# AdaLN-conditioned feed-forward layer on one core: first batch's chain in another order, first weight group halved, small vectors loaded as rows, token parameters on GpSimd

## The reference

```python
attn_in = jnp.tanh(jnp.einsum('bsd,da->bsa', hidden, W1) + b1)     # A = 128
scores = jnp.einsum('bsa,a->bs', attn_in, v)
mask = jnp.where(pt == 0, l <= j, jnp.where(pt == 1, l >= j, l != j))
p = softmax(where(mask, scores[:, None, :], -1e30))
pooled = jnp.einsum('bjl,bld->bjd', p, hidden) / mask.sum(-1)
h = (pooled - mu) * rsqrt(var + 1e-5) * ln_gamma + ln_beta
y = silu(h @ w1 + fc1_bias)          # w1 = (fc1_q - 128) * scales, 512 x 2048
z = y @ w2 + fc2_bias                # w2 = (fc2_q - 128) * scales, 2048 x 512
out = x + pooled + 0.5 * z
```

## Time and profile before

| | us |
|---|---|
| median of 3 runs | 1687.94 |
| lowest, highest | 1685.69, 1688.06 |
| profiled execution | 1684.57 |
| its span in the profile | 1682.8 |
| TensorE busy | 1644.5 (98%) |
| VectorE busy | 931.1 (55%) |
| ScalarE busy | 422.6 (25%) |
| GpSimd busy | 177.6 (11%) |

### The profile page before, as it was taken

How to read it: one execution, slowest core, us unless ns; L and a number is a source line. 1 busy time by engine, 2 the same in 40 slices (tenths; PEclk the granted TensorE clock), 3 DMA queues, 4 the chain that set the end, 5 groups by cost and what they waited for, 6 DMA issues and landing times.

```text
span 1682.8 us, 20819 instructions
## 1 busy us (share of the span) xinstructions
PE 1644.5 (98%) x7648; PEld 1310.1 (78%) x7648; DVE 931.1 (55%) x1827; ACT 422.6 (25%) x632; POOL 177.6 (11%) x140
## 2 busy tenths in 40 slices
PE   4699999999999999999999999999999999999999
PEld 2578878787887878878788787878878788787887
DVE  8887464655546565464564546555365554645612
ACT  2442232223122232222222222231221322222210
POOL 1202010020200102011020200102011020110200
PEclk7799999999999999999999999999999999999999
DMA  9500001010010100101000010100101001010000
GB/s 271 191 1 24 27 1 50 1 51 1 1 52 0 51 1 1 52 1 51 1 33 19 1 50 1 52 1 1 51 1 52 1 1 51 1 51 1 26 0 26
DMA packets 29679, 52.39 MB, mean 31 GB/s; under 512 B 5888, under 2 KB 6400, under 8 KB 29056
## 3 DMA queue, kind: packets, MB, share of 16 engines
q1 hardware_dynamic: 28608, 50.62, 9.1%
q10 hardware_dynamic: 960, 0.27, 0.1%
HBM read 34.10 MB, written 16.78 MB: 30 GB/s over the span
## 4 chain that ended last, share of the span: by engine, by line
PE 95%; DVE 3%; DMA 1%; issue 0%; ACT 0%; SPq 0%; DVEq 0%
PE z_ps L826 14%; PE z_ps L827 14%; PE z_ps L828 14%; PE y_ps L813 14%; PE y_ps L814 14%; PE y_ps L815 14%; PE a_ps L797 2%; PE a_ps L719 2%; PE a_ps L736 1%; DMA fc_scaled<-in_L_ffn_fc_scales_dram 1%; PE a_ps L789 1%; PE a_ps L738 1%; PE a_ps L786 1%; PE a_ps L737 1%; PE a_ps L788 1%; PE a_ps L787 1%
## 5 line engine op out<-in xcount | busy, mean ns | idle before, releaser
L826 PE MATMUL z_ps<-w_hi,y_hi 128*128 128x512 f32 x1024 | 418.9, 409 | 0.0
L813 PE MATMUL y_ps<-hT_hi,w_hi 128*128 128x512 f32 x1024 | 406.2, 397 | 3.0 <-DVE hT_lo L629 2.7
L827 PE MATMUL z_ps<-w_lo,y_hi 128*128 128x512 f32 x1024 | 406.9, 397 | 0.0
L828 PE MATMUL z_ps<-w_hi,y_lo 128*128 128x512 f32 x1024 | 403.6, 394 | 0.0
L814 PE MATMUL y_ps<-hT_lo,w_hi 128*128 128x512 f32 x1024 | 402.9, 394 | 0.0
L815 PE MATMUL y_ps<-hT_hi,w_lo 128*128 128x512 f32 x1024 | 401.3, 392 | 0.0
L412 ACT ACTIVATE y_f<-y_ps,b 128x512 f32<-128x512 f32 x256 | 176.0, 687 | 884.9 <-PE y_ps L815 884.9
L652 DVE CAST y_hi<-y_f 128x512 fp32r<-128x512 f32 x256 | 120.2, 469 | 269.0 <-PE z_ps L828 222.2
L826 PEld LDWEIGHTS z_ps<-w_hi,y_hi 128*128 128x128 f32 x1024 | 192.5, 188 | 61.6 <-issue 19.2
L813 PEld LDWEIGHTS y_ps<-hT_hi,w_hi 128*128 128x128 f32 x1024 | 192.7, 188 | 49.5 <-issue 3.7
L828 PEld LDWEIGHTS z_ps<-w_hi,y_lo 128*128 128x128 f32 x1024 | 192.3, 188 | 46.5
(11 more groups left out here) (142 smaller groups left out, 1146.2 us busy)
## 6 DMA issues: line engine op xcount, KB each, us to landing
x<-in_x_dram SPq DMA_DIRECT2D x64, 256.0 KB, 3.6
out_dram<-x SPq DMA_DIRECT2D x64, 256.0 KB, 2.2
fc_codes<-in_L_ffn_fc_q_dram SPq DMA_DIRECT2D x8, 1024.0 KB, 15.0
fc_scaled<-in_L_ffn_fc_scales_dram SPq DMA_DIRECT2D x8, 1024.0 KB, 16.5
scratch<-in_L_cond_W_dram ACTq DMA_DIRECT2D x1, 256.0 KB, 3.7
b2h<-in_L_ffn_fc_bias_dram SPq DMA_DIRECT2D x1, 256.0 KB, 8.1
tok_i<-in_itok_B_dram ACTq DMA_DIRECT2D x1, 8.0 KB, 5.5
v_col<-in_L_cond_v_dram ACTq DMA_DIRECT2D x1, 0.5 KB, 6.0
```

The lines of the kernel that those rows point to most:

```text
L813: mm(o, w1_hi[:, c, cols], hT_hi[:, c, :], start=(c == 0), stop=False)
L826: mm(z_ps[r][:], y_hi[k % 2][:, rows], w2_hi[:, k, :], start=(k == 0), stop=False)
L827: mm(z_ps[r][:], y_hi[k % 2][:, rows], w2_lo[:, k, :], start=False, stop=False)
L828: last = mm(z_ps[r][:], y_lo[k % 2][:, rows], w2_hi[:, k, :], start=False, stop=(k == NF - 1))
```

## The change

- First batch, x: transposed tile by tile (J) instead of by column block, so that each tile's x^T can be split as soon as it has come. The projection is made in two halves of 256 columns, in two banks, tanh and scores as well. The scans read the scores in PSUM. The scores as a column come from four small matmuls (`score_columns`) instead of a product with the identity.
- First batch, rest: ScalarE makes the high parts of x (XSH), with `xs_hi` and `y_hi` as buffers; the exponential for the sums (EXPE) starts after COLS; the other exponentials in two steps with a semaphore count each, in all batches, and PC's halves release TensorE one by one. h is transposed tile by tile into `z_ps`, and fc1's blocks 0 and 1 are made together, column block by column block (`fc1_first_pair`).
- Weights: five groups, of 2, 2, 4, 4 and 4 blocks (w1 groups 0 to 4, w2 groups 5 to 9). D and W of w1's groups 0 and 1 stand behind the pooling, L of group 0 after H, everything of w2 in the FFN.
- Small vectors: five transfers put gamma, beta, fc1's bias, v and b1 as 26 rows of 128 into `vec_rows`; one transpose and one copy give `vec_cols`.
- Queues: `wc_f` and the tokens move to SyncE, behind x.
- GpSimd makes the token parameters, and `bias` waits for the splits of h (`hT_done`) instead of h.

The diff's core:

```diff
-    NG = NF // ND
+    GROUPS = ((0, 2), (2, 4), (4, 8), (8, 12), (12, 16))
...
-        DVE_LATE = {0: [("D", 1)], 1: [("D", 5)], 2: [("L", 1)], 3: [("D", 2), ("L", 5)], 4: [("D", 6)], 5: [("L", 2)],
-                    6: [("L", 6)], 15: [("D", 3)], 16: [("D", 7)], 17: [("L", 3)], 19: [("L", 7)]}
+        DVE_LATE = {0: [("D", 2)], 1: [("D", 6)], 2: [("L", 2)], 3: [("L", 6), ("D", 7)], 4: [("D", 3)],
+                    5: [("L", 7), ("D", 8)], 6: [("L", 3)], 7: [("L", 8)], 15: [("D", 4)], 16: [("D", 9)],
+                    17: [("L", 4)], 19: [("L", 9)]}
...
             def bias(a, p, J):
                 pool.wait_ge(res_added, a * NJ + (J + 1))
                 if J == 0:
-                    pool.wait_ge(h_ready, a * NJ + NJ)
+                    pool.wait_ge(hT_done, a * ND + ND)
...
-            act.dma_start(wc_f.rearrange("p (c a) -> p c a", c=ND), cond_w.rearrange("(c p) a -> p c a", p=P)).then_inc(wc_in, 16)
-            act.dma_start(tok_i[:], itok.rearrange("(o d) -> o d", o=1).to_broadcast([P, B])).then_inc(tok_in, 16)
-            act.dma_start(v_col[:], cond_v.rearrange("(p o) -> p o", o=1)).then_inc(cond_in, 16)
-            act.dma_start(b1c[:], cond_b.rearrange("(p o) -> p o", o=1)).then_inc(cond_in, 16)
+            rows = [(gamma, 0, ND), (beta, ND, ND), (fc1_b, 2 * ND, NF), (cond_v, 2 * ND + NF, 1), (cond_b, 2 * ND + NF + 1, 1)]
+            for vector, r0, n in rows:
+                act.dma_start(vec_rows[r0:r0 + n, :], vector.rearrange("(c p) -> c p", p=P)).then_inc(rows_in, 16)
...
             def split_pc(a, _, p, ch):
+                dve.wait_ge(exp_done, a * 6 + 5)
+                ch(v.tensor_copy(part_hi[:], p_f))
+                v.tensor_tensor(part_lo[:], p_f, f32(part_hi[:]), ALU.subtract).then_inc(pc_ready, 1)
                 dve.wait_ge(exp_done, a * 6 + 6)
-                ch(v.tensor_copy(part_hi[:], p_f))
-                ch(v.tensor_tensor(part_lo[:], p_f, f32(part_hi[:]), ALU.subtract))
                 ch(v.tensor_copy(coef[:], c_f))
...
             for c in range(ND):
                 split_h(0, c)
+            w_lo_part(1)
+            dequantise(NW)
             ffn(0, 0, True, True)
...
+            def transpose_rows():
+                pe.wait_ge(rows_in, 16 * 5)
+                nc.tensor.transpose(y_ps[1][:, 0:NROWS], vec_rows[:], ident[0:NROWS, 0:NROWS]).then_inc(rows_tr, 1)
...
+            def project_first(n):
+                cols = slice(n * HALF, (n + 1) * HALF)
+                o = (a_ps[1], y_ps[1])[n][:, cols]
+                pe.wait_ge((cond_ready, cols_ready)[n], 1)
+                pe.wait_ge(xt_ready, 2 * (n + 1))
...
+            def fc1_first_pair():
+                pe.wait_ge(w_unit[0], 3)
+                for c in range(ND):
+                    hi, lo = hT_hi[:, c, :], hT_lo[:, c, :]
+                    pe.wait_ge(hT_hi_done, c + 1)
+                    for k in range(2):
+                        cols = slice(k * P, (k + 1) * P)
+                        mm(y_ps[k][:], w1_hi[:, c, cols], hi, start=(c == 0), stop=False)
+                        mm(y_ps[k][:], w1_lo[:, c, cols], hi, start=False, stop=False)
+                    pe.wait_ge(hT_done, c + 1)
+                    for k in range(2):
+                        last = mm(y_ps[k][:], w1_hi[:, c, k * P:(k + 1) * P], lo, start=False, stop=(c == ND - 1))
+                        if c == ND - 1:
+                            last.then_inc(fc1_done, 1)
```

More of the change, by code:

```diff
@@ L157, in build @@
         cond_ready = sem("cond_ready")
-        w_in = [sem(f"w_in{g}") for g in range(2 * ND)]
-        w_unit = [sem(f"w_unit{g}") for g in range(2 * ND)]
+        w_in = [sem(f"w_in{g}") for g in range(2 * NW)]
+        w_unit = [sem(f"w_unit{g}") for g in range(2 * NW)]
         xt_tr = sem("xt_tr")
@@ L416, in w_hi_part @@
                 act.wait_ge(w_unit[g], 1)
-                nc.scalar.activation(hi, wf, ACT.Copy, scale=1.0 if g < ND else 0.5).then_inc(w_unit[g], 1)
+                nc.scalar.activation(hi, wf, ACT.Copy, scale=1.0 if g < NW else 0.5).then_inc(w_unit[g], 1)
             def ffn(b, with_a, first=False):
-                for k in range(2):
-                    silu(b, k)
+                silu(b, 0)
+                if first:
+                    w_hi_part(NW)
+                silu(b, 1)
                 for h in range(LAST):
@@ L480, in _ @@
             link(v.tensor_scalar(row_b[:], row_f[:], -1.0, 1.0, ALU.mult, ALU.add))
+            link(v.tensor_reduce(ident_q[:], ident[:].rearrange("p (q n) -> p n q", n=Q), AX_X, ALU.add))
+            assert done[0] == DVE_CONSTS, done[0]
             dve.wait_ge(wc_in, 16)
@@ L667, in ffn @@
                 split_y(b, 0)
+                if first:
+                    w_lo_part(NW)
                 for h in range(LAST + 1):
@@ L816, in fc1 @@
                 last.then_inc(fc1_done, 1)
+            def fc1_first_pair():
+                pe.wait_ge(w_unit[0], 3)
+                for c in range(ND):
+                    hi, lo = hT_hi[:, c, :], hT_lo[:, c, :]
[9 more added lines that the diff above has]
+                            last.then_inc(fc1_done, 1)
             def fc2(b, k):
-                if is_first(b) and k % NG == 0:
-                    pe.wait_ge(w_unit[ND + k // NG], 3)
+                if is_first(b) and group_from(k) is not None:
+                    pe.wait_ge(w_unit[NW + group_from(k)], 3)
                 pe.wait_ge(split_done, b * NF + (k + 1))
@@ L856, in _ @@
             pe.wait_ge(pool_const, 4)
-            transpose_first_x()
+            transpose_first_x(0)
+            transpose_first_x(1)
+            transpose_rows()
+            transpose_first_x(2)
+            transpose_first_x(3)
+            project_first(0)
+            project_first(1)
+            scores_first(0)
+            scores_first(1)
+            score_columns()
             for name, n in PE_FIRST:
                 steps[name](0, n, 0)
-            for c in range(ND):
-                transpose_h(0, c)
-            fc1(0, 0)
-            fc1(0, 1)
+            for J in range(NJ):
+                transpose_first_h(J)
+            fc1_first_pair()
             ffn(0, 0, True)
```

273 lines of the change are left out of this document (175 added, 98 removed).

## The result

| | us |
|---|---|
| changed kernel, median of 6 runs | 1693.85 (1692.24 to 1696.45) |
| kernel before, the same runs | 1686.00 (1685.39 to 1688.06) |
| ratio, 95% interval | 1.0046 (1.0033 to 1.0059) |
| changed kernel, profiled execution and its span | 1693.73, 1691.9 |

What follows compares the result with a forecast made beforehand. TensorE bounds the 16 batches, so only the start can save: 3.1 + 1.2 + 5.7 + 4.3 - 2.0 = 12.3 us, giving 1675.6 on the median's scale, stated as 1675; range 1669.5 to 1682.

Steps and rivals of the forecast that it cites:

- no wait of TensorE in the loop: Sign for the forecast, in the later batches' loop: TensorE never waits there; waits before each batch's fc2 would prove it wrong.
- a gap of over 2 us with the clock at 0.50 behind it: Sign against the forecast: a TensorE gap of 2 us with a granted clock of 0.50 after 55 us.
- step 4: Normalised tiles to fc2's first matmul: 13.4 us where it was 17.7, saving 4.3, mark at 54.9.
- slower: Rival, later batches: GpSimd's bias pass holds VectorE for all of its 5.72 us in each turn; 1697 us, chance 0.04.
- Step 1: Start up to the first scan: mark at 16.8 us where it was 19.88, saving 3.1.
- the first small rival: Projection's weights land late, at 10.7 us, moving each mark up to the FFN by 2.7; 1678 us, chance 0.10.
- Step 2: Scans to the last exponential argument: 8.6 us where it was 9.8, saving 1.2, mark at 25.4.
- Step 3: Arguments to the last statistics, where it was 17.1 us: saving 5.7, mark at 36.8.
- The weights' term: Ahead of fc2's first matmul: weight steps and y's split, in turns with GpSimd's four additions, done at 54.4, 0.5 to spare.
- the second small rival: First feed-forward part: GpSimd's four additions delay VectorE 1.0 each and the clock falls; some 4 us lost, 1679.5, chance 0.11.
- Step 5: First feed-forward part, fc2's first matmul to fc1's seventh block: VectorE falls behind, 2.0 us lost.
- The last rival: Later batches' bias pass meeting output additions, holding VectorE 5.72 us per turn: 1697, chance 0.04; the forecast took zero.

Runs made afterwards that it cites:

- e1: Changed kernel with 16 empty instructions (satisfied waits) on TensorE's queue ahead of its first transposes: 1673.73 us, ratio to the kernel before 0.9926.
- e11: Changed kernel with 16 empty instructions ahead on TensorE's queue, run once more: 1672.32 us, ratio to the kernel before 0.9925.
- e3: Changed kernel with GpSimd's bias additions of every batch but the first waiting on the normalised tiles again: 1693.32 us, ratio to the kernel before 1.0044.
- e6: Changed kernel with 16 empty TensorE instructions ahead and the first batch's bias additions waiting for the low part of w2's fourth group: 1670.68 us, ratio 0.9901.
- e5: Changed kernel with the loop's 256 KB stores and loads replaced by 32-byte transfers, most output left out: 1686.14 us, ratio to the kernel before 0.9999.
- e4: Kernel before with 34 empty instructions on TensorE's queue ahead of its first transposes: 1690.52 us, ratio to the kernel before 1.0024.
- e2: Kernel before with 49 empty instructions on TensorE's queue ahead of its first transposes: 1708.12 us, ratio to the kernel before 1.0129.
- e7: Changed kernel with 6 empty instructions ahead on TensorE's queue: 1700.46 us, ratio to the kernel before 1.0084.
- e8: Changed kernel with 10 empty instructions ahead on TensorE's queue: 1673.92 us, ratio to the kernel before 0.9926.

## Why the prediction was wrong

**The step that failed** is the sentence on which the sum was carried to the end: "what is saved at the last mark is saved at the end, unless the later batches change", with "After that nothing differs but the batches' own work". For what might change in later batches only the bias pass was looked at. That the change puts 49 instructions ahead of TensorE's loop, which can be counted, and that the place of the loop's code has a price, did not enter. It is worth +20.2 us. Of the signs named beforehand it is "no wait of TensorE in the loop" that this breaks; the other one, a gap of over 2 us with the clock at 0.50 behind it, came at 55.94 and belongs to step 4 below. With the head elsewhere (e1), the change gives 1673.73 where 1675.0 was forecast, and 12.4 us where 12.3 were. So the sum was good for what it covered, and the sign of the answer came from outside it. That the two agree within 0.1 is luck: in e1's trace 10.5 us are saved at the end of the loop's first pass (460.00 for 470.45) and 11.3 over the span (1671.5 for 1682.8), in e11's 12.2 and 12.3. None of the rivals was this one. The rival "slower" had a time near the measured one, 1697 for 1693.85, by another mechanism, the bias pass in each turn, and e3 shows that this has no part in it.

Point by point, marks as predicted and as measured in the changed kernel:

| step | predicted | measured |
|---|---|---|
| 1, first scan | 16.8 | 16.52 |
| 2, arguments end | 25.4 | 24.41 |
| 3, last statistics end | 36.8 | 35.28 |
| 4, fc2's first matmul | 54.9 | 55.94 |
| 5, fc1's seventh block ends | about 84.3 | 85.6 |

Step 1: the projection's weights were there at 7.1 and not at 8.0, which took the first small rival away; the little vectors and the token parameters cost nothing, as taken. Step 2: two scans out of PSUM took 1.23 and 1.22, no more than from SBUF, and the arguments came 7.9 us after the scan for 8.6 estimated. Step 3 took 10.9 for 11.4 estimated.

Step 4 hit its mark within 1.0 by two errors of opposite sign. TensorE was ready at 52.7, earlier than thought, since in this execution the clock was at its upper level through the pair of fc1 blocks (0.23 from start to start). The weights' term, "in turns with GpSimd's four additions they are done at 54.4", was the mis-sized one: it was done at 55.88. The steps before it add up to 53.4, so the sum had charged one encounter of about 1.0. There were four, of 1.1 (2.31 for 1.22), 1.1 (1.51 for 0.43), 1.0 and 1.1. So the mechanism of the second small rival came true, a wait of 3.23, and behind it some eight matmuls at 0.43, 1.6 us; of its price of 4 us, 1.3 stand at the last mark (85.6 for 84.3). e6 shows what it was worth at the end, 3 us. Step 5 lost 2.3 (13.3 saved at its start, 11.0 at its end) for 2.0 counted.

The last rival, GpSimd against the output additions, was rightly given little. (In its working 369.9 and four encounters of 1.0 make 373.9 and not 374.2, and y comes at 375.1, ahead of the 375.32 that it has to meet.) In the changed kernel they meet at each turn, here the one from batch 3 to 4 (order of time of VectorE, then GpSimd, answers to the earlier trace rows):

```profile
356.39 2.48 DVE L735 TENSOR_TENSOR x<-z_ps,x 128x512 f32<-128x512 f32 x4 [0.32 <-PE z_ps L952]
...
360.40 1.66 DVE L726 TENSOR_TENSOR y_lo<-y_f,y_hi 128x512 fp32r<-128x512 f32 x1
```

```profile
356.21 5.30 POOL L361 TENSOR_TENSOR x<-x,b2h 128x512 f32<-128x512 f32 x4 [22.12 <-DVE hT_lo L701]
```

Four additions of a PSUM and an SBUF tile take 2.48 beside GpSimd as they did without it; the low part with two SBUF inputs takes 1.66 for 0.69. The Trainium skill, SBUF — State Buffer, Who interferes with whom, says that a VectorE instruction with at most one SBUF input, outside the two-port modes, does not contend with GpSimd, and that one with two SBUF inputs does. The trace agrees with both, by 2.48 and by 1.66. The prediction had cited the page and had no row for such an addition beside GpSimd.

## What to carry to other kernels

A change ahead of a hardware loop can cost time inside it, because it moves the loop's code. Count the instructions per engine ahead of the loop, and look behind each back edge for idle time without a releaser ("issue") before any other explanation of a loss that comes once per pass; a handful of empty instructions is both the test and the cure. A sum over the start of a kernel may only be carried to its end if the loop's own pass is known to be the same. And where a second engine's instructions have been seen to hold up those of the one that others wait for (GpSimd and VectorE here, 1.0 to 1.1 us each time), charge one encounter for each of them, then move that work to where nobody waits.

## What the runs showed of the hardware

- During a taken branch TensorE goes on with 16 or 17 matmuls issued ahead, 3.9 us at 0.23 (15 to 17 in e5), so that a branch record of 3.7 to 4.1 us costs next to nothing by itself: at 4.09, in the kernel before, the next matmul starts 0.52 behind the last instead of 0.23 (474.20 to 474.72).
- The next 16 KB of instructions after the target's block can be used 3.1 to 4.2 us after the engine resumes (e4, e2, the changed kernel), and up to 4.6 where next to nothing of the head is in the target's block (e7, 461.87 to 466.51). Without other transfers at that time it was 3.1 to 3.4 (e5). From 57 instructions left upward no stall was seen, at 23 it was 0.7 to 0.8 us, at 8 with the transfers 2.1 to 3.2, at 2 it was 3.4 to 4.6.
- Of the fifteen stalls of 2.1 to 3.2 us in the changed kernel, e2 and e3, twelve were followed by a fall of the granted clock, some 1.2 to 1.6 us more. The other three (3.16, 2.85, 2.57) are those at each kernel's first back edge; why, is open. Behind the stalls of e7 the clock fell five times of five, behind those of about 2 us in e5 once, behind those of 0.8 in e4 never.
- The clock's level in the start differs between executions of nearly the same code: through the pair of fc1 blocks it was at the upper level in the changed kernel, and at 0.55 of full speed from 46 to 50 us in e8, with a shorter wait ahead of fc2 (1.07 for 3.23) and the same median as e1.
- Open: why the second block is not asked for together with the first, and whether the loops of the other engines have the same cost where their work is not waited for. Neither was tried.
